# Routed up-projection: six of eight chunks in rounded products, and the second shared W2 loaded earlier

## The reference

```python
sh = _gelu(jnp.einsum('td,sdh->sth', xf, sW1) + sb1[:, None, :])     # 2 shared experts
shared = jnp.einsum('sth,shd->std', sh, sW2) + sb2[:, None, :]
shared = shared.mean(axis=0)
gates = xf @ rW + rb
topk_vals, topk_idx = jax.lax.top_k(gates, TOP_K)                    # 2 of 8 experts
topk_probs = jax.nn.softmax(topk_vals, axis=-1)
h = _gelu(jnp.einsum('td,edh->eth', xf, W1) + b1[:, None, :])        # W1 is 1024 x 256
y = jnp.einsum('eth,ehd->etd', h, W2) + b2[:, None, :]               # W2 is 256 x 1024
moe = jnp.einsum('te,etd->td', w, y)
```

## Time and profile before

| | |
|---|---|
| median of 3 runs | 327.25 us (326.6 to 327.38) |
| the profiled execution's own time | 327.5 us |
| its span, first to last instruction | 325.8 us |
| TensorE busy | 315.9 us (97%) |
| VectorE busy | 245.6 us (75%) |
| ScalarE busy | 192.5 us (59%) |
| granted TensorE clock | 1.00 throughout |
| DMA | 57.62 MB, mean 177 GB/s |

### The profile page before, as it was taken

The page is one execution under the profiler, slowest core; times in us unless marked ns, Lnnn a source line. Parts: engine busy times, 40 slices in busy tenths (PEclk is TensorE's granted clock), DMA queues, the critical chain, the costliest instruction groups (busy, mean ns, idle before and its releaser), DMA issues.

```text
span 325.8 us, 6188 instructions
## 1 busy us (share of the span) xinstructions
PE 315.9 (97%) x2006; PEld 275.0 (84%) x2006; DVE 245.6 (75%) x474; ACT 192.5 (59%) x321; POOL 78.7 (24%) x94
## 2 busy tenths in 40 slices
PE   6999999999999999999999999999999999999996
PEld 2889897788899988888999888888988888878885
DVE  2999999988768666874665779977877787582885
ACT  2896999997122424442156889788878777650000
POOL 6741090001010110120213334322324430004800
PEclk9999999999999999999999999999999999999999
DMA  7970014000001126489052684989998973225975
GB/s 247 357 198 1 3 17 159 2 3 15 2 0 67 64 94 211 149 272 364 11 189 66 234 281 153 322 294 313 374 340 288 323 311 129 91 103 188 343 309 188
DMA packets 27012, 57.62 MB, mean 177 GB/s; under 512 B 2733, under 2 KB 16537, under 8 KB 26980
## 3 DMA queue, kind: packets, MB, share of 16 engines
q1 hardware_dynamic: 20452, 33.89, 30.9%
q0 software_dynamic: 3888, 14.16, 12.8%
q10 hardware_dynamic: 2640, 9.17, 7.1%
HBM read 66.25 MB, written 14.03 MB: 246 GB/s over the span
## 4 chain that ended last, share of the span: by engine, by line
PE 71%; ACT 10%; DVE 6%; issue 4%; DMA 4%; DVEq 2%; SPq 1%; ACTq 0%
PE ps L1581 46%; PE ps L1878 10%; PE ps L1867 5%; DMA y_acc<-in_x 4%; PE ps L1710 4%; ACT arena_r L782 2%; DVEq L1168 2%; PE ps L1591 2%; DVE work L1152 2%; DVE big L1165 1%; ACT sw_raw L847 1%; PE ps L1745 1%; PE ps L1891 1%; ACT xt L763 1%; PE ps L1957 1%
## 5 line engine op out<-in xcount | busy, mean ns | idle before, releaser
L1581 PE MATMUL ps<-arena_r 128*128 128x512 f32 (+3 forms) x300 | 74.2, 391 | 0.4 <-DVE arena_r L1458 0.3
L1581 PEld LDWEIGHTS ps<-arena_r 128*128 128x128 f32 (+1 forms) x300 | 53.0, 187 | 12.1 <-issue 0.8
L1581 PE MATMUL ps<-xt,arena_r 128*128 128x314 f32 (+3 forms) x324 | 60.3, 337 | 0.0
L1581 PE MATMUL ps<-arena_r,xt 128*128 128x286 f32 (+1 forms) x360 | 59.0, 305 | 0.4 <-DVE arena_r L559 0.3
L679 POOL DMA_INDIRECT big<-xrow,tok_i x17 | 36.7, 2161 | 89.1 <-PE ps L1867 70.4
L1581 PEld LDWEIGHTS ps<-xt,arena_r 128*128 128x128 f32 (+1 forms) x324 | 51.2, 187 | 5.5 <-issue 0.3
L1581 PEld LDWEIGHTS ps<-arena_r,xt 128*128 128x128 f32 (+1 forms) x360 | 49.2, 187 | 1.5 <-DVE arena_r L559 0.6
L1463 DVE TENSOR_TENSOR arena_r<-raw,arena_r 128x2048 fp32r<-128x2048 f32 x17 | 38.8, 2285 | 0.4 <-ACT arena_r L1029 0.2
L1878 PE MATMUL ps<-big,tile 128*128 x160 | 37.4, 380 | 0.2 <-issue 0.2
L1029 ACT ACTIVATE arena_r<-raw 128x2048 fp32r x17 | 32.4, 1903 | 0.8 <-issue 0.7
L1878 PEld LDWEIGHTS ps<-big,tile 128*128 128x128 f32 x160 | 29.1, 190 | 3.7 <-issue 0.4
(11 more groups left out here) (244 smaller groups left out, 472.2 us busy)
## 6 DMA issues: line engine op xcount, KB each, us to landing
big<-in_L_ffn_W SPq DMA_DIRECT2D x19, 1024.0 KB, 7.4
raw<-in_L_ffn_W SPq DMA_DIRECT2D x19, 1024.0 KB, 10.8
yrow<-work ACTq DMA_DIRECT2D x17, 512.0 KB, 4.4
raw<-in_L_gnn_W_rel SPq DMA_DIRECT2D x2, 1144.0 KB, 10.7
y_acc<-in_x SPq DMA_DIRECT2D x4, 512.0 KB, 8.3
xrow<-work SPq DMA_DIRECT2D x4, 512.0 KB, 2.9
raw<-in_L_ffn_sW SPq DMA_DIRECT2D x2, 1024.0 KB, 5.8
sw_raw<-in_L_ffn_sW SPq DMA_DIRECT2D x2, 1024.0 KB, 11.4
```

What stands on the lines that cost most here:

```text
L1581: ins = pe.matmul(out_ap, a, b, start=start and k == 0, stop=stop and k == n - 1)
```

## The change

- `FK`, the number of rounded chunks in tiles 2 to 15, goes from 4 to 6. The parts get separate places: the rounded W1 of six chunks, its rest for the first four (`w1_lo_v`) and for the last two (`w1_lo_p`, in a part of `xt` that was free).
- ScalarE's two row copies are cut at 256 and 768 columns instead of 512 and 512. `w1_hi` becomes two copies, of four chunks (`r_w1hi`) and of two (`r_w1top`); `w1_lo` two subtractions, the second with its own semaphore `r_w1rest`. VectorE makes all of the rests.
- TensorE no longer takes the three products chunk by chunk: first all six rounded by rounded, then all rests of the rows by rounded W1, then rounded rows by the rests of W1, four and two; each group waits for its own part.
- `load_sw2(1)` stands in SyncE's turn 6 (`SW2_LOAD`) instead of turn 13. Where it is split and used stays.

```diff
--- before.py
+++ after.py
@@ -111,14 +111,23 @@
         xt_flat = xt[:, :, :, :].rearrange("p a k n -> p (a k n)")
         sw2_hl = [[xt_flat[:, (2 * e + i) * UNIT:(2 * e + i + 1) * UNIT]
                    .rearrange("p (k n) -> p k n", k=KH) for i in range(2)] for e in range(NS)]
-        FK = KD // 2
+        FK, FV = 6, 4
         ROUNDED = range(2, NT - 1)
+
+        def rounded_upto(i):
+
+            return sum(1 for n in ROUNDED if n <= i)
+
         split_at = 2 * UNIT
-        w1_hl = [xt_flat[:, split_at + i * FK * HID:split_at + (i + 1) * FK * HID]
-                 .rearrange("p (k n) -> p k n", k=FK) for i in range(2)]
-        split_at += 2 * FK * HID
+        w1_hi_t = xt_flat[:, split_at:split_at + FK * HID].rearrange("p (k n) -> p k n", k=FK)
+        split_at += FK * HID
+        w1_lo_v = xt_flat[:, split_at:split_at + FV * HID].rearrange("p (k n) -> p k n", k=FV)
+        split_at += FV * HID
         xg_hl = [xt_flat[:, split_at + i * FK * P:split_at + (i + 1) * FK * P] for i in range(2)]
         assert split_at + 2 * FK * P <= 2 * NS * UNIT
+        top_at = 2 * NS * UNIT + D
+        w1_lo_p = xt_flat[:, top_at:top_at + (FK - FV) * HID].rearrange("p (k n) -> p k n", k=FK - FV)
+        assert (FK - FV) * HID <= NP
         B_GAP = 32
         KB = 2 * B_GAP + NX
         b2_hl = xt_flat[0:KB, 2 * NS * UNIT:2 * NS * UNIT + D]
@@ -395,6 +404,8 @@
         r_xlo = sem("r_xlo")
         r_w1hi = sem("r_wonehi")
         r_w1lo = sem("r_wonelo")
+        r_w1top = sem("r_wonetop")
+        r_w1rest = sem("r_wonerest")
         r_ya = sem("r_yact")
         r_c = sem("r_c")
         r_h = sem("r_h")
@@ -411,7 +422,7 @@
         s_out = sem("s_out")
 
         NG, NLN = 5, 3
-        SW2_HALVES, SW2_AT = (1, 2), NT - 3
+        SW2_HALVES, SW2_LOAD, SW2_AT = (1, 2), 6, NT - 3
         LAST_COLS = (slice(0, DH), slice(DH, DH + DH // 2), slice(DH + DH // 2, D))
         NLO = NG - 2
         U_SW1, U_SW2 = NLO, NLO + NS
@@ -520,7 +531,7 @@
                     sp.wait_ge(r_w2lo, free)
                 sp.dma_start(raw[:, bass.ds(ring * SLOT, UNIT)].rearrange("p (k n) -> p k n", k=KH),
                              w2v[bass.ds(e, 1)].rearrange("e p k n -> (e p) k n"), cond=new).then_inc(s_w2[i % NS_W], 16)
-                if i == SW2_AT - 1:
+                if i == SW2_LOAD:
                     load_sw2(1)
 
             for t in range(T - 1):
@@ -741,10 +752,6 @@
         def down_bank(i):
             return ps[3 if i % 2 else 0]
 
-        def rounded_upto(i):
-
-            return sum(1 for n in ROUNDED if n <= i)
-
         def block_of(b):
             return b // 2, b % 2
 
@@ -976,8 +983,9 @@
 
                 act.wait_ge(r_t, i + 1)
                 if i in ROUNDED:
-                    act.activation(xg_t[:, FK * P:], ps[2][:, 1, :], ACT.Copy)
-                    act.activation(xg_hl[0], ps[2][:, 0, :], ACT.Copy).then_inc(r_x, 1)
+                    rows = ps[2][:, :, :].rearrange("p a n -> p (a n)")
+                    act.activation(xg_t[:, FK * P:], rows[:, FK * P:], ACT.Copy)
+                    act.activation(xg_hl[0], rows[:, 0:FK * P], ACT.Copy).then_inc(r_x, 1)
                 else:
                     act.activation(xg_t, ps[2][:, :, :].rearrange("p a n -> p (a n)"), ACT.Copy).then_inc(r_x, 1)
 
@@ -985,8 +993,10 @@
 
                 act.wait_ge(s_w1[i % NS_W], 16 * (i // NS_W + 1))
                 act.wait_ge(r_u, i)
-                act.activation(w1_hl[0], big[:, bass.ds(ring * UNIT, FK * HID)].rearrange("p (k n) -> p k n", k=FK),
-                               ACT.Copy).then_inc(r_w1hi, 1)
+                act.activation(w1_hi_t[:, 0:FV], big[:, bass.ds(ring * UNIT, FV * HID)]
+                               .rearrange("p (k n) -> p k n", k=FV), ACT.Copy).then_inc(r_w1hi, 1)
+                act.activation(w1_hi_t[:, FV:FK], big[:, bass.ds(ring * UNIT + FV * HID, (FK - FV) * HID)]
+                               .rearrange("p (k n) -> p k n", k=FK - FV), ACT.Copy).then_inc(r_w1top, 1)
 
             def keep_y_act(i):
 
@@ -1475,13 +1485,18 @@
             def rows_t_lo(i):
 
                 dve.wait_ge(r_x, i + 1)
-                dve.tensor_tensor(xg_hl[1], ps[2][:, 0, :], xg_hl[0].bitcast(F32), ALU.subtract).then_inc(r_xlo, 1)
+                dve.tensor_tensor(xg_hl[1], ps[2][:, :, :].rearrange("p a n -> p (a n)")[:, 0:FK * P],
+                                  xg_hl[0].bitcast(F32), ALU.subtract).then_inc(r_xlo, 1)
 
             def w1_lo(i, ring):
 
                 dve.wait_ge(r_w1hi, rounded_upto(i))
-                dve.tensor_tensor(w1_hl[1], big[:, bass.ds(ring * UNIT, FK * HID)].rearrange("p (k n) -> p k n", k=FK),
-                                  w1_hl[0].bitcast(F32), ALU.subtract).then_inc(r_w1lo, 1)
+                dve.tensor_tensor(w1_lo_v, big[:, bass.ds(ring * UNIT, FV * HID)].rearrange("p (k n) -> p k n", k=FV),
+                                  w1_hi_t[:, 0:FV].bitcast(F32), ALU.subtract).then_inc(r_w1lo, 1)
+                dve.wait_ge(r_w1top, rounded_upto(i))
+                dve.tensor_tensor(w1_lo_p, big[:, bass.ds(ring * UNIT + FV * HID, (FK - FV) * HID)]
+                                  .rearrange("p (k n) -> p k n", k=FK - FV),
+                                  w1_hi_t[:, FV:FK].bitcast(F32), ALU.subtract).then_inc(r_w1rest, 1)
 
             def keep_u(i):
 
@@ -1878,10 +1893,19 @@
                     ins = pe.matmul(o, xg_t[:, k * P:(k + 1) * P], big[:, bass.ds(ring * UNIT + k * HID, HID)],
                                     start=k == first, stop=k == KD - 1 and first == 0)
                 if i in ROUNDED:
+                    x_hi, x_lo = (x.rearrange("p (k n) -> p k n", k=FK) for x in xg_hl)
+                    pe.wait_ge(r_w1top, rounded_upto(i))
+                    for k in range(FK):
+                        pe.matmul(o, x_hi[:, k], w1_hi_t[:, k], start=False, stop=False)
                     pe.wait_ge(r_xlo, rounded_upto(i))
+                    for k in range(FK):
+                        pe.matmul(o, x_lo[:, k], w1_hi_t[:, k], start=False, stop=False)
                     pe.wait_ge(r_w1lo, rounded_upto(i))
-                    ins = hilo(o, [((xg_hl[0][:, k * P:(k + 1) * P], xg_hl[1][:, k * P:(k + 1) * P]),
-                                    (w1_hl[0][:, k], w1_hl[1][:, k])) for k in range(FK)], start=False)
+                    for k in range(FV):
+                        pe.matmul(o, x_hi[:, k], w1_lo_v[:, k], start=False, stop=False)
+                    pe.wait_ge(r_w1rest, rounded_upto(i))
+                    for k in range(FV, FK):
+                        ins = pe.matmul(o, x_hi[:, k], w1_lo_p[:, k - FV], start=False, stop=k == FK - 1)
                 ins.then_inc(r_u, 1)
 
             def tile_hidden(i):
```

## The result

The changed kernel is **slower**, by 1.1%: 330.74 us, the median of four runs (329.96 to 330.93), against 326.98 us of the kernel before beside them (326.6 to 327.38); ratio 1.011, 95% interval 1.0089 to 1.0132. That is +3.8 us, where +1.9 was forecast.

A forecast was written before the change was run, and what follows sets the result against it. The prediction took TensorE's work, 7.04 us a tile, to bound the routed loop. A 2.0 us saving and 3.9 us lost to the moved load gave +1.9 us, 329.1 us on the 327.25 median; range 326.8 to 331.4.

The forecast's parts named there:

- Direction and chain: SyncE's queue: the moved load waits until about 208, W1 of tile 7 issues at 211.2; slower, loss over 3 us, chance 0.62.
- TensorE's saving: Rounded tiles 2 to 15: 72 ns per chunk that changes sides, 0.144 us a tile, 2.0 us in all.
- VectorE, ScalarE and the order: Inside each tile: VectorE gets +0.9 us, ScalarE 0.63 us; both fit, with some 0.6 us left, at cost 0.
- the cover: New product order wants the first weight rest only 2.3 us into the tile; in tile 6, 1.3 us of lateness is covered.
- tile 7: W1 of tile 7 lands at 218.4; TensorE waits 0.3 us, then 0.8 for ScalarE's rounding: loss 1.1 us.
- tile 8: W1 of tile 8 lands at 227.3; TensorE waits 1.2 us, then 0.8 for the rounding: loss 2.0 us.
- tile 9: W2 of tile 8 lands at 231.7 and holds ScalarE; TensorE waits 0.5, plus about 0.3 for VectorE's rests: loss 0.8 us.
- The sum of bytes: DMA landings of late loads: bytes queued, shared W2 included, at 354 GB/s plus 1.4 us lag; W1 of tile 7 at 218.4.
- 1: Rival on the loads of tiles 7 and 8: they come in time, all 2.0 us gained, 325.2 us; chance 0.10.
- 2: Rival on DMA rate: near 390 GB/s the loss is 1.6 us, nearly balanced, 326.9 us; chance 0.18.
- 3: Rival: VectorE's work passes TensorE's 6.9 us in the 14 tiles, 2.8 us on top of the forecast, 331.9 us; chance 0.05.
- 4: Rival: TensorE's rounded chunks are no cheaper in the new order, the saving is gone, 331.1 us; chance 0.05.

The follow-up runs named there:

- first profile: The changed kernel itself, unaltered, as profiled with the result: 330.74 us against 326.98 for the kernel before; its profiled span 328.9 us, with the clock fall.
- experiment 3: Changed kernel with the shared load back in turn 13 but SyncE's wait for it left in turn 6: 330.82 us against 327.7 for the kernel before, ratio 1.0103.
- experiment 8: Six rounded chunks, load in turn 13, but products in the old chunk-by-chunk order behind one wait: 339.1 us against 327.48 for the kernel before, ratio 1.0353.
- experiment 1: Changed kernel with the second shared W2 load back in turn 13, so rounded chunks and new order alone: 325.96 us against 327.7 for the kernel before, ratio 0.9948.
- second profile: The changed kernel run once more, unaltered, for the clock: 330.02 us against 326.65 for the kernel before; span 327.9 us, clock at 1.00.
- experiments 2 to 6: Kernel before with load in turn 6, 1.0108; changed kernel with SyncE's wait alone in turn 6, 1.0103, in turn 7, 1.0045; ScalarE issuing load, 1.0077; load in turn 7, 0.9959.
- experiment 4: Changed kernel with the load in turn 13 and SyncE's wait in turn 7 behind the table reads: 328.57 us against 327.48 for the kernel before, ratio 1.0045.

## Why the prediction was right, and where it was not

**Direction and chain: right.** SyncE's wait at 208.1, the table reads behind it and W1 at 211.1 are seen to a tenth, all of TensorE's new waits in the first profile lie between 217 and 231, tile 10 loses nothing, and experiment 3 shows that this wait makes the loss. (TensorE's listed waits add up to 3.3 us where some 4 were to show; the starts of the tiles show the whole.)

**TensorE's saving: right.** 72 ns a chunk, 6.90 us a tile. The Trainium skill's isolated gap (TensorE: Matmul & The Clock Gate, Back-to-back issue gap), which by the prediction's estimate would have given 2.8 us and a pitch of 6.84, is not what the trace shows. That estimate left the gap's 2.5 ns out of the full chunk's four passes; with them it is 437 ns a chunk, a saving of 3.1 us, and further off.

**VectorE, ScalarE and the order: right.** A tile of VectorE grew from 5.47 us (5.44 of 7.00 in the earlier trace rows, by 7.04) to 6.41 (6.50 by 6.90): +0.94, forecast 0.9. Experiment 8 shows that the cover is needed in every tile, and what it is worth (0.90 us). It was over-rated: in tile 6, for which 1.3 us of it were to be left, the first rest ends at 211.36 + 1.21 = 212.57 and its products start at 213.18, 0.6 us later.

**Size of the loss: too small.** Forecast 3.9 us, in the tiles 5.4 and 4.5 in two profiles, some 5.5 between the medians of the changed kernel and of experiment 1, each against its kernel before. So the whole change cost 3.8 us where 1.9 was forecast. Term by term (a tile's share is its late start and what its own products lose up to the transposes behind them, which they reach after 3.02 us undisturbed; tile 8's in the first profile is taken up to its rounded products, since from there on the clock is half):

| | forecast | first profile | second profile |
|---|---|---|---|
| tile 7 | 1.1 | 0.69 + 0.78 = 1.47 | 0.75 + 0.76 = 1.51 |
| tile 8 | 2.0 | 1.86 + 0.68 = 2.54 | 1.92 + 0.60 = 2.52 |
| clock at half | not foreseen | 1.42 | 0 |
| tile 9 | 0.8 | 0 | 0.42 |
| sum | 3.9 | 5.43 | 4.45 |

Tile 7's term was right in its cause and small by 0.4. W1's landing at 218.4 was right; TensorE would have been there at 210.88 + 6.90 = 217.8, not at 218.1, since what lies ahead of the loop was 0.35 us shorter here. That gain was only waited away. In **tile 8 the step that failed** is "W1 of tile 8 ... lands at 227.3: waits 1.2". That W1 was there when ScalarE came to it, at 227.75. What was late was W2 of tile 7 (224.0), which the forecast left out; but ScalarE stood at it in its order, with b2, due in this very turn, behind it, ahead of tile 8's row copies. The forecast used this same mechanism one tile later, for W2 of tile 8, whose landing it had right (231.7; 231.76 seen). For tile 7 its own count of bytes leaves it open whether the term would have been seen: an estimate of 221.4 with 1.05 MB behind W1, from which no wait follows, and 224.3 with a second gather and store as well. In tile 9 the first profile has no wait; in the second its products stand 0.42 us for VectorE's rests, which is the forecast's "about 0.3 for VectorE's rests". The clock was not in the forecast at all.

**The sum of bytes: the right moment, partly by luck.** The shared megabyte was counted ahead of W1 at 354 GB/s, 3.0 us. Experiment 3 has no megabyte there and the same landing, so the bytes were not on the path. They filled just the 3.0 us in which SyncE read its table, and counted from W1's own issue the sum comes out the same: 211.07 + 1.4 + 2.1 MB / 0.354 = 218.4. The rate itself was uneven: 334 GB/s from 211 to 218, then 396 to 420, above the 390 that was taken as the upper end. That end came of which stretches were picked; the kernel before shows more one microsecond beside the fastest of the earlier trace rows:

```profile
231.00:238.00 7.00, 7.00 (x43) 6.21 (x43) 5.59 (x7) 5.44 (x9) 2.53 (x2) 1.00 1.04 408
```

At such a rate throughout, the forecast's own sum would have shrunk to under 1.6 us of loss. A rate put too low for what came behind 218 and a load left out worked against each other, and the range held because it was wide: its upper end stood for 317 GB/s, which is not what made the time. The Trainium skill (DMA: Bandwidth & Descriptors, Bandwidth) gives 425 GB/s for 16 MB read by one core alone; the highest of the stretches shown, 420 over 4.4 us of mixed traffic, lies just below it.

**Rivals.** 1 and 2 fell (a loss of 4.4 us or more in the tiles). 3 fell: in experiment 1 no up product waits for VectorE; the short waits for W1's rests in the second profile (tile 9) and in experiments 2 to 6 come behind late loads. 4 fell: experiment 1's tiles take 6.90 us, where rounded chunks that are no cheaper would have left them at 7.04. That left the forecast with its 0.62, and it was the case that came.

## What to carry to other kernels

Before you move a DMA's issue, read what its wait holds up on the queue of its issuer: a load that waits for a late buffer costs the loads behind it, and the table reads behind it too, even when it moves nothing. Put it behind the loads that are wanted (turn 8 here), not ahead. And a late operand must be followed through every engine that handles it in order: the one that no product of its own tile wanted yet held the engine that made the next operand.

## What was not expected of the hardware

- The granted clock fell to 0.52 for 3.6 us behind a wait of 1.7 us and stayed at 1.00 behind waits of 1.6, 1.8 and 2.0 us, the second in the same kernel. In the kernels whose TensorE didn't wait no execution showed a mean clock below 0.999; among the twelve runs of experiment 4, five had 0.994 or 0.995, with spans of 327.8 to 328.4 us against 324.0 to 326.6 of the others. How much of that is the clock's own cost is not shown.
- The DMA engines at a full share moved anything from 317 GB/s (206 to 213 us in the kernel before) to 420 (225 to 229.4 in the changed one). The high rates need no backlog: the kernel before has 417 GB/s from 232.4 to 236.8. What sets the rate at a full share is not shown.
- With a backlog, SyncE's issue of a single load took 2.53 us (at 217.07), where it takes 0.39 otherwise, and what stands behind it on SyncE comes that much later. The other three profiles with the standing queue in turn 6 and six rounded chunks show 2.48 to 2.61; that a full queue holds the issuer back is a guess.
